# Expert stages of a four-layer network on one core: tiles stay in their PSUM bank up to the low part, VectorE makes every low part

## The reference, cut to what matters

```python
# m0: 8 experts of 256, m2: 160 experts of 64 and a shared one
out = x + sum_e share[t, e] * (act(x @ w1[e]) @ w2[e])
# m1: 64 experts of 64 and a shared one of 128 (gated)
h = silu(einsum('th,eih->eti', x, eg_w)) * einsum('th,eih->eti', x, eu_w)
routed = einsum('eti,ehi,te->th', h, ed_w, comb)
```

## Time and profile before

| | us |
|---|---|
| median of 3 runs (2387.32 to 2389.07) | 2387.56 |
| the profiled execution | 2387.65 |
| its span in the trace | 2385.8 |
| in it: experts of m0, about | 302 to 408 |
| experts of m1, about | 636 to 937 |
| experts of m2, about | 1141 to 1617 |

### The profile page before, as it was taken

How to read it: one execution, slowest core, us unless ns; L and a number is a source line. 1 busy time by engine, 2 the same in 40 slices (tenths; PEclk the granted TensorE clock), 3 DMA queues, 4 the chain that set the end, 5 groups by cost and what they waited for, 6 DMA issues and landing times. The chain is left out here.

```text
span 2385.8 us, 50677 instructions
## 1 busy us (share of the span) xinstructions
PE 1873.4 (79%) x16799; PEld 1167.7 (49%) x16806; DVE 1893.2 (79%) x3977; ACT 1354.8 (57%) x3451; POOL 546.9 (23%) x490
## 2 busy tenths in 40 slices
PE   6999787576688887585899999995777686774987
PEld 5999633454333333364333333334455354443775
DVE  4444579788799998587899999997777877886776
ACT  5666467334354544553777777775455554653555
POOL 1000143000355553101455555550000000000000
PEclk7555689788699999797999999997988887885785
DMA  2000095100365662000999999980000000000000
GB/s 73 4 4 4 11 191 118 37 1 0 82 143 132 140 135 50 15 1 11 205 202 202 201 202 202 204 181 15 14 0 13 13 0 13 13 0 28 2 1 19
DMA packets 53549, 172.00 MB, mean 72 GB/s; under 512 B 9136, under 2 KB 34352, under 8 KB 36784
## 3 DMA queue, kind: packets, MB, share of 16 engines
q1 hardware_dynamic: 52272, 168.40, 31.8%
q10 hardware_dynamic: 1152, 1.90, 0.3%
HBM read 165.75 MB, written 2.95 MB: 71 GB/s over the span
## 5 line engine op out<-in xcount | busy, mean ns | idle before, releaser
L810 ACT ACTIVATE m_hwhi<-m_hw 128x512 f16<-128x512 f32 x523 | 326.9, 625 | 209.9 <-DVE m_hw L855 209.8
L836 DVE TENSOR_TENSOR m_hwlo<-m_hw,m_hwhi 128x512 f16<-128x512 f32 x362 | 395.9, 1094 | 0.2
L816 ACT ACTIVATE m_h<-ps 128x512 f32<-128x512 f32 x520 | 308.9, 594 | 74.3 <-PE ps L774 62.7
L747 POOL TENSOR_TENSOR m_hwlo<-m_hw,m_hwhi 128x512 f16<-128x512 f32 x167 | 231.7, 1388 | 456.4 <-ACT m_hwhi L810 407.0
L855 DVE TENSOR_TENSOR m_hw<-m_h,m_comb 128x512 f32<-128x512 f32 x388 | 316.1, 833 | 20.0 <-DMA m_comb<-m_shares 11.3
L780 PE MATMUL ps<-m_hwhi,m_whi 128*128 128x512 f16 x532 | 204.8, 385 | 87.7 <-DVE m_hwlo L836 87.2
L774 PE MATMUL ps<-x_hi,m_whi 128*128 128x512 f16 x652 | 248.9, 382 | 5.2 <-ACTq L805 5.2
L774 PE MATMUL ps<-x_lo,m_whi 128*128 128x512 f16 x652 | 248.8, 382 | 0.0
L774 PE MATMUL ps<-x_hi,m_wlo 128*128 128x512 f16 x652 | 248.6, 381 | 0.0
L780 PE MATMUL ps<-m_hwlo,m_whi 128*128 128x512 f16 x532 | 203.0, 382 | 0.0
L780 PE MATMUL ps<-m_hwhi,m_wlo 128*128 128x512 f16 x532 | 202.8, 381 | 0.0
(11 more groups left out here) (423 smaller groups left out, 4655.9 us busy)
## 6 DMA issues: line engine op xcount, KB each, us to landing
m_comb<-m_shares SPq DMA_DIRECT2D x256, 512.0 KB, 6.4
m_stage<-in_m_w SPq DMA_DIRECT2D x97, 128.0 KB, 6.0
m_stage<-in_m_w SPq DMA_DIRECT2D x33, 192.0 KB, 6.1
lj_w<-in_lj_w SPq DMA_DIRECT2D x6, 768.0 KB, 4.3
lq_w<-in_lq_w SPq DMA_DIRECT2D x1, 1536.0 KB, 5.9
la_w<-in_la_w SPq DMA_DIRECT2D x1, 1280.0 KB, 5.4
rn_rows<-in_L_attn_rows SPq DMA_DIRECT2D x4, 256.0 KB, 4.0
rn_xs<-rn_xn_hi SPq DMA_DIRECT2D x32, 32.0 KB, 2.0
```

Of the source, the lines that this page charges most:

```text
L747: nc.gpsimd.tensor_tensor(hw_lo[:, slot, :], hw[:, n, :], hw_hi[:, slot, :], ALU.subtract)\
L810: nc.scalar.activation(hw_hi[:, k % HB, :], hw[:, n, :], ACT.Copy).then_inc(hi_done, 1)
L816: nc.scalar.activation(h[:, k % 2, :], gate_bank(k), func).then_inc(act_done, 1)
L836: nc.vector.tensor_tensor(hw_lo[:, slot, :], hw[:, n, :], hw_hi[:, slot, :], ALU.subtract)\
```

## The change

In all three expert stages:

- Tile k's bank goes through all steps. Activation (m0, m2), product with `h` (m1) and product with the shares are written back to the bank where the product was made; high and low part are read from it. `hu` and `hw` in SBUF are gone, `h` is kept for m1. The gate product of m1 always uses bank 4, the up products banks 5 to 7 in turn (`NB` = 3); m0 and m2 use banks 4 to 7 in turn (`NB` = 4).
- A bank is taken for tile k when the low part of tile k - NB is done (`wait_low(pe, at, gone)`); the order low part of k - 2 behind the product of k on VectorE stays.
- `ON_POOL` is empty: VectorE makes all low parts. GpSimd only splits weights.
- Both rows of a unit's shares come in one transfer over 128 partitions.
- The first body is written out on its own (`each_body`), without waits for what isn't there yet. Zeroing, the head start of semaphores, and unit 0's down products are gone.

```diff
-    AHEAD = 2 if gated else 4
-    LAG = 4
+    LAG = NQ
     HB = 2 * UB
-    ON_POOL = (1, 3) if gated else (1,)
+    NB = 3 if gated else 4
+    ON_POOL = () if gated else ()
...
+    def bank(k):
+        return ps[:, 8 - NB + k % NB, :]
+
+    def acted(k):
+        return h[:, k % 2, :] if gated else bank(k)
+
+    def weighted(k):
+        return hw_pool[:, k % NQ, :] if k % NQ in ON_POOL else bank(k)
...
+            def spread(row, s):
+                many = 2 if halves else 1
+                sp.dma_start(comb[:, s, :], route.rows[bass.ds(row, many)].unsqueeze(1)
+                             .broadcast_to([many, P // many, N])).then_inc(comb_got[s], 16)
...
+            def body(at, turn, first):
+                for k in range(NQ * UB):
+                    s, n = k // NQ, k % NQ
+                    if n == 0:
+                        pe.wait_ge(split_done, at(s, 1, 1))
+                    if gated:
+                        if not first or k > 0:
+                            pe.wait_ge(act_done, at(s, NQ, n))
+                        product(ps[:, 4, :], slice(0, P), s, n).then_inc(gate_done, 1)
+                    if not first or k >= NB:
+                        gone = k - NB
+                        if gone % NQ in ON_POOL:
+                            pe.wait_ge(hw_done, at(gone // NQ, NQ, gone % NQ + 1))
+                        else:
+                            wait_low(pe, at, gone)
+                    if gated:
+                        product(bank(k), slice(P, 2 * P), s, n).then_inc(up_done, 1)
+                    else:
+                        product(bank(k), slice(0, P), s, n).then_inc(gate_done, 1)
+                    if not first or k >= LAG:
+                        wait_low(pe, at, k - LAG)
+                        down(k - LAG)
...
+            def body(at, turn, first):
+                for k in range(NQ * UB):
+                    s, n = k // NQ, k % NQ
+                    dve.wait_ge(act_done, at(s, NQ, n + 1))
+                    if gated:
+                        dve.wait_ge(up_done, at(s, NQ, n + 1))
+                        nc.vector.tensor_tensor(bank(k), acted(k), bank(k), ALU.mult).then_inc(hu_done, 1)
+                        dve.wait_ge(hu_done, at(s, NQ, n + 1))
+                    if n == 0:
+                        dve.wait_ge(comb_got[s], turn(16))
+                    if n in ON_POOL and (not first or s > 0):
+                        wait_low(dve, at, k - NQ)
+                    nc.vector.tensor_tensor(weighted(k), bank(k), comb[:, s, n * QW:(n + 1) * QW], ALU.mult)\
+                        .then_inc(hw_done, 1)
+                    if (n - 2) % NQ in ON_DVE and (not first or k >= 2):
+                        low(at, k - 2)
```

More of the change, by code:

```diff
@@ L717, in _ @@
             for s in range(1 if halves else 0, UB):
[L718 to L722, removed]
+                spread(2 * (s - 1) if halves else s // 2, s)
+            with sp.Fori(0, U // UB - 1) as j:
                 for s in range(UB):
-                    sp.wait_ge(split_done, j * UB + (UB + s + 1))
+                    sp.wait_ge(split_done, j * UB + (s + 1))
@@ L776, in product, with down @@
                 return last
-            def down(s, n, slot):
+            def down(k):
                 for a, b in ((w_hi, hw_hi), (w_hi, hw_lo), (w_lo, hw_hi)):
[L780 to L796, removed]
@@ L801, in _ @@
+            each_body(pe, body)
+            for k in range(NQ * (U - 1), NQ * U):
+                wait_low(pe, fixed, k)
+                down(k)
         @block.scalar
@@ L803, in _, with high, body @@
             route.scalar(act)
[L804 to L821, removed]
+            nc.scalar.activation(warm[:], S.ident[:, 0:1], func)
+            def high(k):
+                nc.scalar.activation(hw_hi[:, k % HB, :], weighted(k), ACT.Copy).then_inc(hi_done, 1)
+            def body(at, turn, first):
+                for k in range(NQ * UB):
+                    s, n = k // NQ, k % NQ
+                    act.wait_ge(gate_done, at(s, NQ, n + 1))
+                    nc.scalar.activation(acted(k), ps[:, 4, :] if gated else bank(k), func).then_inc(act_done, 1)
+                    if not first or k > 0:
+                        act.wait_ge(hw_done, at(s, NQ, n))
+                        high(k - 1)
+            each_body(act, body)
+            act.wait_ge(hw_done, NQ * U)
+            high(NQ * U - 1)
+            act.wait_ge(down_done, NQ * U)
             for n in range(NQ):
@@ L827, in _ @@
             route.vector(dve)
[L828 to L836, removed]
-                    .then_inc(lo_dve, 1)
[L839 to L858, removed]
-                            low(j * UB + (s if n < 2 else s + 1), m, (k - 2) % HB)
```

91 lines of the change are left out of this document (42 added, 49 removed).

## The result

| | us |
|---|---|
| before, median of 4 runs (2387.32 to 2391.18) | 2388.32 |
| changed kernel, median of 4 runs (3920.17 to 3929.92) | 3922.69 |
| ratio, 95% interval | 1.6426 (1.6398 to 1.6455) |
| profiled execution of the changed kernel, its span | 3923.11, 3921.3 |

The kernel became slower by 64%. The forecast had the sign and missed the size: it said 2484, with a range of 2445 to 2535.

The account below looks back on a forecast made before the run. VectorE was taken to set the pace, stretched by GpSimd. From 2387.6 us: +101.9 for bank waits in m1, -1.9 and -1.4 in m2 and m0, -2 for dropped idle matmuls, giving 2484 us, range 2445 to 2535.

Parts of the forecast that it names:

- The pace of before and what stretched VectorE: Before: 2.282 us a tile in m1, 1.466 m2, 1.482 m0; GpSimd stretches VectorE operations with two SBUF inputs.
- The ring of m1: In m1 up(k + 3) waits for low(k), one tile in the loop: 3.06 us a tile against 2.282, +101.9 us.
- The rings of m0 and m2: Bank waits there span two tiles: 2.92 us for two, 1.46 a tile; -1.9 us in m2, -1.4 in m0.
- Writes to a PSUM bank, taken as nothing: ScalarE or VectorE writing a bank: no row shows it, bounded at 0.15 us each, two per ring, counted as nothing.
- side sum of 26 us for m1: Cost in m1 if each VectorE operation on PSUM took some 65 ns more: 131 x 0.195; not counted.
- Both rows in one transfer, "costed at nothing": Shares of a unit in one transfer: same bytes, 1.18 MB a unit at 202 GB/s against 218 possible; no cost.
- slower, the single transfer: Rival, chance 0.05: transfer rate 15% lower, 186 GB/s, units of m0 and m2 take 6.35 us, 49 more, 2533.
- cover it: Shares are asked for two units, 11 us at 5.8 each, before they are needed, which was said to suffice.
- The sign, slower with 0.90: The whole kernel becomes slower, chance 0.90; faster 0.08, within 0.2% of before 0.02.
- Slower, clock lost in m1 (0.09): Rival, chance 0.09: TensorE's clock stays at 1.2 GHz in m1, 3.87 us a tile, 106 us more, 2590.
- Faster, the bank's wait doesn't bind (2296): Rival, chance 0.08: m1 at 1.94 us a tile, m2 and m0 at 5.41 us a unit, 2296 us.
- 218 if full: DMA rate in GB/s at full load, taken from 198 GB/s at a share of 0.91 in the windows before.

Follow-up runs that it names:

- experiment 8: The kernel before with only ON_POOL emptied, so VectorE makes every low part and tiles stay in SBUF; 2322.19 us, ratio 0.9721.
- experiment 2: The changed kernel with a unit's shares in two transfers again, one row over 64 partitions each; 2466.11 us.
- experiment 4: The changed kernel with expert rows in turn on the partitions, one transfer with 64 steps outermost and the two rows inside; 2455.22 us, ratio 1.0278.
- experiment 6: The changed kernel with two transfers over 64 partitions each and VectorE's low part of tile k - 1, not k - 2; 2302.72 us, ratio 0.9639.
- experiment 7: The changed kernel with rows in turn in one transfer and the low part one tile behind, not two; 2267.52 us, ratio 0.9498.

## Why the prediction was wrong

**The pace of before and what stretched VectorE:** right. With its operations on a bank all stay narrow, and GpSimd's cast of the weights runs at its own pace (shortest, median, longest ns), first in the changed kernel, then in that of experiment 8:

```profile
L844 DVE TENSOR_TENSOR m_hwlo<-ps,m_hwhi x520: 678/680/683, 312.5 to 3151.0; 128x512 f16<-128x512 f32 x174
...
L757 POOL CAST m_whi<-m_stage x130: 396/398/505, 285.0 to 3123.4; 128x256 f16<-128x256 f32 x97, 128x384 f16<-128x384 f32 x33
```

```profile
L756 POOL CAST m_whi<-m_stage x130: 395/832/1499, 292.6 to 1537.5; 128x256 f16<-128x256 f32 x97, 128x384 f16<-128x384 f32 x33
```

**The ring of m1:** right, 3.06 us forecast, 3.00 after where no shares are waited for, 2.99 in experiment 2. The link from the up product's last matmul to the product with `h` was 0.49 us (804.19 to 804.68) in place of 0.57; the others came within 0.02. Experiment 2 gives +92.9 for m1 where the term was +101.9.

**The rings of m0 and m2:** the mechanism held, the size was a little off. 1.42 us a tile in both (m0: 89.3 / 63) against 1.46, so -14.6 in m2 and -2.5 to -4 in m0 where -1.9 and -1.4 stood. The three stages of experiment 2 add up to 2388.4 + 92.9 - 14.6 - 2.5 = 2464, and it measured 2466. So with the shares in two transfers the forecast of 2484 would have been 18 us too high, and inside its range.

**Writes to a PSUM bank, taken as nothing:** nearly. The multiply took 699 ns at the median (L859) against 682, the product with `h` 697 against 675: 0.02 us each. The prediction's side sum of 26 us for m1 (131 x 0.195) charges three operations, though the product with `h` read a bank before as well; two of the three would make 17. The two steps that it would have lengthened were 0.73 and 0.60 us in the changed kernel (801.68 to 802.41 to 803.01), as before within 0.02.

**Both rows in one transfer, "costed at nothing": this step failed.** It compared bytes, 1.18 MB at 202 GB/s against 218, and left a margin of 7% for the case that "the one transfer ran" less well, as if only the number of transfers changed. What changed was the shape: the row index became the slowest dimension, with size 2. Two DMA engines of 16 carried it. The real rate was 51 GB/s for the shares, a quarter, and a unit took 20.3 us in m2 (1642.8 / 80.75) where 5.84 stood: +278 us in m1 (670.1 - 391.9) and +1184 in m2 (1642.8 - 458.8). The rival "slower, the single transfer" named the right part of the change, and its sign in the profile (VectorE waiting for `m_comb`) was the one seen, but it had a chance of 0.05 and no mechanism, and its rate, "15% lower", came from no row. What bore on it was at hand, the shape in the diff: `[many, P // many, N]` with many = 2. And the two units, 11 us, that "cover it" were an argument on latency; when every unit's transfer takes 20 us, starting each one 11 us earlier doesn't help.

**The sign, slower with 0.90:** not luck, but a small part of what was measured. The rings of banks that it rested on make 78 of the 1535 us.

**Slower, clock lost in m1 (0.09):** not by the ring: 1.00 in experiments 2 and 4. The 0.67 to 0.78 in the changed kernel follow the long stops and aren't their cause. TensorE in m2, behind a wait of 12.55 us, begins with matmuls of 0.61 to 0.63 us, the 1.2 GHz duration, and is back at 0.38, that of 2.4 GHz, later in the unit:

```profile
2000.39 0.61 PE L776 MATMUL ps<-x_hi,m_whi 128*128 128x512 f16 x1 [12.55 <-DVE m_hwlo L844]
2000.80 0.63 PE L776 MATMUL ps<-x_lo,m_whi 128*128 128x512 f16 x1
...
2005.75 0.38 PE L776 MATMUL ps<-x_lo,m_whi 128*128 128x512 f16 x1
```

It costs little there: VectorE waits for the next shares until 2019.62, whatever TensorE's speed.

**Faster, the bank's wait doesn't bind (2296):** false as a forecast, since the ring binds, but its arithmetic is what experiment 6 reached by opening the ring: 1.94 us a tile in m1 as it said, 5.49 us a unit in m2 where it had 5.41, 2302.7 in all.

## What to carry to other kernels

A transfer is priced by its shape before its bytes: write down its outermost dimension and compare a transfer of the same shape in the trace; an outermost dimension of two left 14 of 16 DMA engines idle for most of the time, and the page then shows a low DMA share with everyone waiting for a transfer. When a buffer is held longer, close the ring from its release back to its next use and count how many tiles it spans; a ring of one tile set the pace here with no engine full, and moving one instruction by one tile opened it. And when a change has several parts, run each alone: here the transfer's shape cost 61%, and the other parts, with one instruction moved and the rows in turn, gave 5%. The part that moved all low parts to VectorE gave 2.8% by itself.

## What the runs showed of the hardware

- A transfer of two rows to 128 partitions with the rows outermost ran at 51 GB/s, on two DMA engines (two packets under way for 94% of the time); with the same rows in turn it ran in bursts of 406 to 446 on 16. With 51 pairs outermost three engines worked. A DMA engine moved about 26 GB/s in all three (8 KB in 0.309 to 0.314 us).
- Two transfers over 64 partitions each kept the 16 engines busy for 0.95 at 207 GB/s, one over 128 partitions for 0.58 at the same rate, since a packet of the former took 0.629 us and one of the latter 0.309. The "218 if full" of the prediction was the limit of the shape, not of the DMA engines: experiment 7 moved 234 GB/s at 0.64.
- With the transfers backed up, issuing one on SyncE's queue took up to 13 to 18 us, so a slow transfer also delays unlike ones behind it: weights landed after 41.9 us at the median, and after 6.0 in the kernel before.
- GpSimd's cast and VectorE's operations with both inputs in SBUF stretched each other (cast 832 ns at the median in experiment 8, 398 beside operations on a bank in the changed kernel), and none of VectorE's three operations on a bank went beyond 700 ns.
- Still open: whether the last 55 us of experiment 7 over experiment 8 need the banks.
